# Choice of experts in five pieces in the head of the second attention, the drain of the first in another order, later weights at other addresses

## The reference, cut to what matters

```python
# first attention: 16 heads, delta rule (state += k * beta*(v - k.state)), then
x = x + _L0_attn_ref(xn, ...) + _L0_ffn_ref(xn, ...)      # the latter: 2 of 8 experts for each token
xn = _layernorm(x, axis=-1)
# second attention: for each chunk of 64 tokens, for each sequence and head
gate = ki @ w0_; hb = ki @ w2_; hidden = silu(gate) * hb
dhidden = vi @ w1_.transpose(0, 2, 1)
w1g = newtonschulz5(einsum(hidden * lr1i, vi))            # two steps: A = X X'; B = bA + cAA; X = aX + BX
w0g = newtonschulz5(einsum(ki * lr0i, silu_backprop(dhidden * hb, gate)))
w2g = newtonschulz5(einsum(ki * lr2i, dhidden * silu(gate)))
# w += wg, columns scaled back to their first norms; oi = silu(qi @ w0_) * (qi @ w2_) @ w1_
# lr0, lr1, lr2 = softplus(x @ W_lr + b_lr + const)
# second feed-forward part
gate_probs = softmax(x.mean(axis=1) @ gate_W.T)           # 8 x 6
topk_vals, topk_idx = top_k(gate_probs, 2); topk_vals /= topk_vals.sum()
```

## Time and profile before

| | us |
|---|---|
| median of 3 runs | 1823.56 (1822.08 to 1824.55) |
| the profiled execution | 1825.56 |
| its span, first to last instruction | 1823.8 |
| TensorE busy | 1708.1 (94%) |
| VectorE busy | 1491.5 (82%) |
| ACT busy | 1199.8 (66%) |
| GpSimd busy | 1102.9 (60%) |

### The profile page before, as it was taken

The page is one execution under the profiler, slowest core; times in us unless marked ns, Lnnn a source line. Parts: engine busy times, 40 slices in busy tenths (PEclk is TensorE's granted clock), DMA queues, the critical chain, the costliest instruction groups (busy, mean ns, idle before and its releaser), DMA issues.

```text
span 1823.8 us, 41456 instructions
## 1 busy us (share of the span) xinstructions
PE 1708.1 (94%) x14070; PEld 1242.4 (68%) x14070; DVE 1491.5 (82%) x3496; ACT 1199.8 (66%) x2907; POOL 1102.9 (60%) x1148
## 2 busy tenths in 40 slices
PE   5999899999999999999999999999988778888878
PEld 4477557777777777677777767777767566666666
DVE  4422499999999999999999999999976688888843
ACT  1124467777777777777777777777753678777853
POOL 1510057777777777766666666666666568777831
PEclk8999999999999999999999999999986899999989
DMA  9323300110110101100001000000002000000032
GB/s 308 132 94 110 109 22 27 36 34 26 29 35 20 38 26 29 38 17 26 23 17 29 23 17 23 27 14 29 15 1 59 1 1 2 1 1 1 9 87 81
DMA packets 66096, 73.83 MB, mean 40 GB/s; under 512 B 10975, under 2 KB 54767, under 8 KB 65775
## 3 DMA queue, kind: packets, MB, share of 16 engines
q1 hardware_dynamic: 62919, 63.92, 12.1%
q0 software_dynamic: 3072, 8.65, 1.5%
HBM read 55.45 MB, written 17.10 MB: 40 GB/s over the span
## 4 chain that ended last, share of the span: by engine, by line
PE 83%; DVE 8%; ACT 5%; issue 2%; POOL 1%; SPq 1%; DMA 0%; ACTq 0%; POOLq 0%; DVEq 0%
PE banks L731 19%; PE banks L874 6%; PE banks L743 4%; PE banks L830 3%; PE banks L751 3%; PE banks L849 3%; PE banks L759 3%; PE banks L788 3%; PE banks L802 3%; PE banks L684 3%; PE banks L796 2%; PE banks L930 2%; PE banks L795 2%; PE banks L703 2%; PE banks L1006 2%
## 5 line engine op out<-in xcount | busy, mean ns | idle before, releaser
L731 PE MATMUL banks<-xnT,hw 128*128 128x512 f32 x768 | 414.8, 623 | 4.0 <-DVE cv L2011 4.0
L2052 DVE CAST_PREDICATED MM<-lmask,banks 128x512 bf16<-128x512 uint32 x384 | 270.9, 705 | 36.8 <-PE banks L796 32.3
L2011 DVE SCALAR_TENSOR_TENSOR cv<-banks,hc,cv 128x510 f32<-128x510 f32 (+2 forms) x384 | 283.6, 739 | 11.1 <-ACT cv L1427 6.4
L1477 ACT ACTIVATE T<-banks 128x256 bf16<-128x256 f32 x384 | 150.2, 391 | 144.8 <-PE banks L788 142.9
L2648 POOL TENSOR_TENSOR X<-X,yrow 128x512 f32<-128x512 f32 x128 | 163.4, 1277 | 68.4 <-ACT yrow L1509 68.4
L2612 POOL TENSOR_TENSOR kn<-nsum,half_pos 128x4 f32<-128x4 f32 x64 | 65.5, 1023 | 147.9 <-DVE nsum L2023 147.9
L796 PEld LDWEIGHTS banks<-MM,T 128*128 128x128 bf16 x1536 | 104.2, 98 | 64.4 <-issue 48.0
L795 PEld LDWEIGHTS banks<-T,MM 128*128 128x128 bf16 x1280 | 99.1, 97 | 65.4 <-ACT T L1477 63.2
L788 PEld LDWEIGHTS banks<-MM,Gb 128*128 128x128 bf16 x1536 | 79.1, 98 | 93.6 <-DVE MM L2052 54.5
L874 PE MATMUL banks<-ho,OT 128*128 128x256 f32 x512 | 142.7, 402 | 0.0
L2011 DVE SCALAR_TENSOR_TENSOR cv<-banks,hcv,cv 128x510 f32<-128x510 f32 (+2 forms) x192 | 140.9, 734 | 1.3 <-ACT cv L1427 1.2
(11 more groups left out here) (318 smaller groups left out, 4891.0 us busy)
## 6 DMA issues: line engine op xcount, KB each, us to landing
MM<-in_eye SPq DMA_DIRECT2D x64, 256.0 KB, 2.7
slot_rows<-zeros SPq DMA_DIRECT2D x1, 5304.0 KB, 21.0
xs<-slot_rows SPq DMA_DIRECT2D x13, 408.0 KB, 4.0
slot_out<-ye SPq DMA_DIRECT2D x13, 384.0 KB, 2.7
hw<-in_hw SPq DMA_DIRECT2D x16, 256.0 KB, 3.5
wT<-in_winit SPq DMA_DIRECT2D x8, 384.0 KB, 4.4
wgu<-in_wgu SPq DMA_DIRECT2D x1, 2816.0 KB
w1c<-in_ew SPq DMA_DIRECT2D x16, 176.0 KB
```

The costliest lines, as they stand in the source:

```text
L731: ins = pe.matmul(PROJ[t][:], hw[:, kk, t, :], xnT[:, kk, u.b * BLK:(u.b + 1) * BLK], start=(kk == 0), stop=(kk == KD - 1))
L1477: act.activation(strips(T1[:].rearrange("p i t -> p (i t)"), LEVELS[lv], 0, 1), grams_bank(u)[:, 0:TILES * 64].rearrange("p (k e) -> p k e ...
L2011: dve.scalar_tensor_tensor(o, y, taps_of(t)[:, TAPS - 1 - i:TAPS - i], o, ALU.mult, ALU.add).then_inc(dve_conv, 1)
L2052: dve.copy_predicated(dst, m, ps).then_inc(dve_mm, 1)
```

## The change

Five things are changed.

1. `choose_experts` is cut into `choose_probabilities`, `choose_ranks`, `choose_expert(k)` and `choose_weights`. They are called in the head, among the last VectorE lines before the loop over `pair_period`, and no longer in the loop.
2. ACT's exponential and the Silu behind it become `gate_exponentials`, called between `keep_v(x1)` and `keep_hidden(x1)`; before, they stood last in the head, behind `keep_total(x1)`.
3. The order of the drain and the head is another in some places on all four engines.
4. The weights of pairs 2 and 3 are laid out over buffers of the first attention in another order, and `MM`, `T1` stand behind `hw`, `hc`, `hcv` in memory.
5. SyncE waits for `outputs` and for the squares of unit a62, not for a63, before `load_weights(2)`; the wait for `pe_y` before `load_weights(3)` is gone.

```diff
-        MM = asb("MM", [P, NBLK, 2, TILES, P], BF16)
-        T1 = asb("T1", [P, TILES, P], BF16)
         hw = asb("hw", [P, KD, 3, HD])
         hc = asb("hc", [P, 2, TAPS])
         hcv = asb("hcv", [P, 1, TAPS])
+        T1 = asb("T1", [P, TILES, P], BF16)
+        MM = asb("MM", [P, NBLK, 2, TILES, P], BF16)
...
-        places = [(1, small + early), *((p, small + passing + lasting) for p in range(2, NP)), (1, late), (0, small + passing + lasting), (1, lasting)]
+        places = [(1, small + early), (2, small), (3, these(w02)), (2, turned), (3, small), (2, these(w02) + gated + these(wT) + solved),
+                  (3, turned + gated + these(XX, Bm, w1p)), (3, these(wT, LA)), (1, these(XX)), (0, small + passing + lasting), (1, lasting)]
...
# SyncE
-            sp.wait_ge(pe_solve, 12 * UNITS)
+            sp.wait_ge(pe_solve, 12 * (UNITS - 1))
+            sp.wait_ge(pool_osum, UNITS - 1)
             load_weights(2)
-            sp.wait_ge(pe_y, 2 * UNITS)
             sp.wait_ge(*weights_loaded(2))
             load_weights(3)
# TensorE
             times_gram(a62, 1, 1)
+            project_v(x0)
             invert(a63, 11)
             correct(a62, 1, 1)
             invert(a63, 12)
-            project_v(x0)
             outputs(a62)
# ACT
+            def gate_exponentials():
+                act.wait_ge(*f_lg)
+                act.activation(lge[:], lg[:], ACT.Exp).then_inc(act_once, 1)
+                act.activation(table[:, 1:2], onw[:], ACT.Silu)
...
             square_qk(x0)
+            silu_v(x0)
             invert(a63, 6)
             finish_inverse(a63)
-            silu_v(x0)
...
             keep_qk(x1)
             keep_v(x1)
+            gate_exponentials()
             keep_hidden(x1)
...
             keep_total(x1)
-            act.wait_ge(*f_lg)
-            act.activation(lge[:], lg[:], ACT.Exp).then_inc(act_once, 1)
-            act.activation(table[:, 1:2], onw[:], ACT.Silu)
# VectorE: choose_probabilities, choose_ranks, choose_expert(k), choose_weights hold the steps
# of choose_experts unchanged and in their order
...
             invert(a63, 2)
+            weight_norms()
             second_rhs_half(a62)
             second_rhs(a62)
             invert(a63, 3)
-            weight_norms()
             residual(a62, 1, 0)
             invert(a63, 4)
             refine(a62, 1, 0)
             rates_begin(0)
+            norm_stats(1, 1)
             invert(a63, 5)
             residual(a62, 1, 1)
-            norm_stats(1, 1)
+            sum_qk(x0)
             refine(a62, 1, 1)
-            sum_qk(x0)
             rates_end(0)
+            norm_rows(1, 1)
             residual(a63, 0, 0)
-            norm_rows(1, 1)
+            norm_qk(x0, 0)
             refine(a63, 0, 0)
             square_sums(a62)
             residual(a63, 0, 1)
-            norm_qk(x0, 0)
-            refine(a63, 0, 1)
             norm_qk(x0, 1)
             norm_qk(x0, 2)
+            refine(a63, 0, 1)
             second_rhs_half(a63)
...
             scale(x0, 0)
             scale(x0, 1)
+            choose_probabilities()
             grad_gate(x1)
             grad_hidden(x1)
+            rates_end(3)
             silu_slope(x1)
+            choose_ranks()
             through_silu(x1)
-            rates_end(3)
+            choose_expert(0)
             newton(x0, 0, 0, SQUARE)
+            choose_expert(1)
             sum_qk(x2)
+            choose_weights()
             newton(x0, 0, 0, NEXT)
             norm_qk(x2, 0)
             for n in range(3, STEPS):
                 pair_period(n)
-                if n == 4:
-                    choose_experts()
# GpSimd
             inverse_rms(a62)
+            rate_keys(x0)
             add_rows(a62, 0)
-            rate_keys(x0)
...
             root_grads(x0)
             rate_keys(x1)
+            rate_powers(3)
             one_minus(x1)
             rate_hidden(x1)
-            rate_powers(3)
             root_qk(x2)
```

More of the change, by code:

```diff
@@ L316, in build, with these @@
         lasting = ((wT, "wT", [NM, 4, P], F32), (w02, "w02", [4, 2, P], F32))
-        late = tuple(t for t in passing if t[0] is XX)
-        early = tuple(t for t in passing if t[0] is not XX)
-        places = [(1, small + early), *((p, small + passing + lasting) for p in range(2, NP)), (1, late), (0, small + passing + lasting), (1, lasting)]
+        def these(*group):
+            return tuple(t for g in group for t in passing + lasting if t[0] is g)
+        turned = these(QR, vv, qkT, vT)
+        gated = these(th, sg1, hb1, dgate)
+        solved = these(XX, Bm, w1p, LA)
+        early = these(QR, vv, qkT, vT, th, sg1, hb1, dgate, Bm, w1p, LA)
+        places = [(1, small + early), (2, small), (3, these(w02)), (2, turned), (3, small), (2, these(w02) + gated + these(wT) + solved),
+                  (3, turned + gated + these(XX, Bm, w1p)), (3, these(wT, LA)), (1, these(XX)), (0, small + passing + lasting), (1, lasting)]
         below = [t for p, tensors in places[:-2] for t in tensors]
@@ L2118, in _, with choose_probabilities @@
                     period(h, j)
-            def choose_experts():
-                def by_batch(v):
-                    return v.unsqueeze(2).to_broadcast([1, NB, E1])
+            def choose_probabilities():
                 dve.wait_ge(*f_exp)
@@ L2126, in choose_experts, with choose_ranks @@
                 step(dve.reciprocal(lmx[:], lmx[:]))
-                step(dve.tensor_tensor(lge[:], lge[:], by_batch(lmx[:]), ALU.mult))
+                step(dve.tensor_tensor(lge[:], lge[:], lmx[:].unsqueeze(2).to_broadcast([1, NB, E1]), ALU.mult))
+            def choose_ranks():
                 four = [1, NB, E1, E1]
```

13 lines of the change are left out of this document (7 added, 6 removed).

## The result

The changed kernel takes 1814.53 us, median of six runs (1812.96 to 1817.92); the kernel before, beside it, 1824.05 (1822.08 to 1824.94). The profiled execution took 1812.96 us, with a span of 1811.2 against 1823.8.

What follows compares the result with a forecast made beforehand. The prediction took a closed cycle of waits between engines as the bound, one period lengthened by the choose_experts block. -6.80 (period) + 2.0 (head) - 0.5 (drain) = -5.3 us, from 1823.56 to 1818.3 us; range 1815.0 to 1822.0.

Steps and rivals of the forecast that it cites:

- The period, -6.80: Second attention's periods: taking the choose_experts block out shortens one period from 27.34 to 20.54 us, -6.80 us.
- The 0.84 put down to the lower clock: Part of the period's 6.80 us beyond the 5.96 block: TensorE resuming at its lower clock level, 0.84 us.
- GpSimd and VectorE in the head: Head: GpSimd's earlier power frees rates_end(3), held up 0.95 us beside GpSimd; SQUARE of x0 +1.9, NEXT +3.3 us.
- The table loads: Head, activation engine: loads move behind keep_v(x1), delay keep_hidden(x1) 0.86 us, TURN unchanged; 1.34 us wait for keep_qk(x2) goes.
- The 3.6 us estimated from the Trainium skill's drain: Head: by the skill's load and drain times, two table switches would hold up keep_hidden some 3.6 us; not used in the sum.
- The head costs 2.0 us: Head before the periods: the choice's pieces delay turn_v(x2), and gates(x2) behind it, by 2.0 us.
- slower: Rival: TensorE's longer wait leaves it at 1.2 GHz through head and first periods; +8.5 us, 1832.1; chance 0.03.
- The mark that was set: Sign: keep_v(x1) to project_qk(x3), 32.04 us before; near 34 means the forecast, over 36 costlier-head or slower-clock rivals.
- the first rival: Head hides all the moved work: GpSimd doesn't hold up VectorE, keep_qk's wait pays the rest; -7.0 us, 1816.6; chance 0.17.
- The drain, -0.5: Drain: reordering brings the refinement 0.6 to 0.9 us sooner, then TensorE's queue sets the pace; -0.5 us, bounds -1.2 and +1.2.
- The weights, 0: Weights of pairs 2 and 3: loads issue close to 20 us sooner, but nobody waits for them before or after; 0 us.
- The forecast of -5.3: Whole kernel: period, head and drain terms together, -5.3 us, median to 1818.3 us; forecast 1816.5 to 1820, chance 0.58.

Runs made afterwards that it cites:

- e6: Kernel before with only the exponentials moved early, behind keep_v(x1); the choice of experts stays in the period: 1820.79 us, ratio 0.9985.
- e11: Kernel before, unchanged, profiled once more; no median given, its end behind scale(x15, 0) took 87.47 us.
- e12: Kernel before, unchanged, for a second further profile; no median given, its end behind scale(x15, 0) took 84.19 us.
- e1: Kernel before with only the choice of experts, the exponentials and rates_end(3)/rate_powers(3) moved as in the change: 1819.61 us, ratio 0.9954.
- e3: Changed kernel with SyncE's waits before load_weights(2) and (3) as they were, so the weights load late: 1819.99 us, ratio 0.9961.
- e5: Changed kernel once more, unchanged, beside the kernel before on one chip: 1815.06 us against 1823.78, ratio 0.9958.
- e2: Changed kernel with choice, exponentials and rates_end(3)/rate_powers(3) put back; new drain order, addresses and early weights kept: 1830.08 us, ratio 1.0012.
- e4: Changed kernel with TensorE's products for the first SQUARE of x0 made nine times, filling its wait: 1820.23 us, ratio 0.9960.
- e7: Changed kernel with SQUARE of x0 put ahead of the ranks and both experts: ratio 0.9957 to the kernel before.
- e8: Changed kernel with five more small VectorE steps that do nothing behind pair_period(4): 1814.83 us, ratio 0.9959.
- e13: Kernel before with five small VectorE steps that do nothing behind pair_period(6), putting off its end: ratio 1.0012.
- e14: Kernel before with eight small VectorE steps that do nothing behind pair_period(6), putting off its end: ratio 1.0019.
- e10: Like e9, but with rates_end(3) and rate_powers(3) early as in the change: 1812.81 us, ratio 0.9950.
- e9: Changed kernel with the choice's pieces in VectorE's waits of five periods, rates_end(3)/rate_powers(3) put back: 1811.13 us against 1823.01, ratio 0.9936.

## Why the prediction was right in direction and missed in size

- **The period, -6.80: right.** -6.86 from x3 to x15. This section took 293.15 to 293.28 us in the four profiles that have the block and no added steps or late low stretch (before, e6, e11, e12) and 286.36 to 286.44 in four without it (after, e1, e3, e5). In e2, e4 and e7 a low stretch of the head reaches into the first period and adds 0.9 to 1.1 to it. The 0.84 put down to the lower clock went with the block. e8 and e13 show the same form: a pause of TensorE in the periods, then a low stretch.
- **GpSimd and VectorE in the head: right, a little too dear.** In times of before, `rates_end(3)` starts at 1416.73 (forecast 1416.65) and ends at 1420.3 (1420.5). It was held up by 0.64 instead of 0.95, and not in its chain of seven (1.49) but in three single steps beside `one_minus` and `rate_hidden` (the 0.38, 0.33 and 0.47 above; each took 0.18 before, the first in the earlier trace rows). The ranks, with GpSimd idle, took what they took in the block. The Trainium skill ("GPSIMD Engine Reference", "1. Specifications") names VectorE instructions with two SBUF inputs and those in a 2-port perf mode. Of the three that were held up, the 0.33 has two SBUF inputs; the 0.38 and 0.47 have one, and no run here shows in which mode they ran. SQUARE came +1.48 (forecast +1.9) and NEXT +2.85 (+3.3), the second SQUARE at 1434.13 (1434.3), `gates(x2)` +1.66 (+2.0).
- **The table loads: right.** 2.96 us from the first load to `keep_hidden(x1)`, which is 0.89 later (forecast 0.86); TURN at 1415.20 in times of before (1415.16). The 3.6 us estimated from the Trainium skill's drain ("ScalarE: Activation LUTs", "What ACT_TABLE_LOAD costs") are not there: 0.89 was measured. The wait of 1.34 us for `keep_qk(x2)` is gone.
- **"The head costs 2.0 us": the step that failed.** The way from `gates(x2)` to `project_qk(x3)` was put at no change without a reason: the prediction took `gates(x2)` as the start of the cycle and let what follows be as before. The text had the lower clock as a loss only, in the rival "slower"; it did not ask at which level the kernel before ran its own chain. The earlier trace rows showed 1.00 for the windows up to 1424.7 and from 1441.7 on, and the gap between them, where the low stretch of 1435 to 1441.5 lies, was not looked at. (Of the two slices in the earlier trace rows that the prediction names, the 0.6 is the first.) From `gates(x2)` to `project_qk(x3)` it was 7.73 and became 5.58: -2.15 on the +1.66, so -0.5 for the head. Over five profiles of each (before, e11 to e14; after, e1, e3, e5, e8) the head is 30.60 and 29.99 us on average, -0.6. e6 shows those 2.15 with another cause of the shift, e4 and e7 show 8.30, when the low clock falls there again. Why the low stretches fall where they do stays open. The mark that was set, `keep_v(x1)` to `project_qk(x3)`, is 31.54 against 32.04 before. Under 33 was to mean the first rival; the number is met and its mechanism isn't, since NEXT's delay did reach `gates(x2)`. With e5 and e11 the difference of the heads in a single pair of profiles is anywhere from about -1.5 to +1.1, in no pair +2.0.
- **The drain, -0.5: not settled.** The refinement did come 1.2 us sooner, and `project_qk(x1)` 2.15, counted from the rate bias. But the next matmuls of TensorE need what stands behind GpSimd's power for pair 1, and that was only 0.6 sooner (lines below): TensorE waited 1.72 instead of 0.40, then 3.37 instead of 2.71, and 0.27 was left. Over all nine profiles with the new order (after, e2 to e5, e7 to e10) the drain takes 72.95 to 75.19 us, 74.7 on average with a median of 75.06; over the seven with the old order (before, e1, e6, e11 to e14) 74.99 to 75.40, 75.2 with a median of 75.19. So it is 0.4 by the averages and 0.1 by the medians, and the difference of the two is e4 and e7, which kept more of the lead. The term's path, that TensorE's own queue sets the pace in the end, was not the one that the rows show.
- **The weights, 0: right.** Nobody waits for them in e3 either.
- **The end: no term at all.** -3.80 in the two profiles. The ends with the block in place average 85.3 us (seven executions), those without 83.6 (nine), both reaching from under 84 to over 87. In each the length follows the mean clock: the three ends above 87 us (before, e5, e11) had 0.92, that of e9, 82.28, had 1.00. So most of the 3.8 is luck of the pair of executions. Whether the remaining 1.7 is there on average stays open; e11 to e14 show only that the clock makes it and that the change isn't needed for it.

Put together: -6.9, head about -0.6, drain -0.1 to -0.4, is -7.6 to -7.9. The measured -9.5 has an interval of -11.5 to -6.7, and the other versions with the same lines moved (e1, e3, e5) give -7.8, -7.4 and -8.7. The forecast of -5.3 was short by 2.15 for the clock's part in the head and by small terms; the rest, up to 2 us, is the end, the part ahead of the drain or the spread, and its cause is not shown.

The drain after: VectorE's `refine(a62, 1, 1)`, the last step of `rates_end(0)`, and `norm_rows(1, 1)`, which now stands ahead of the residual (compare); TensorE's wait for that residual (2.72 before); GpSimd's sum of squares beside the last step of `rates_end(0)`.

```profile
1359.84 0.42 DVE L2072 TENSOR_TENSOR Wd<-Wd,banks 128x256 f32<-128x256 f32 x1
...
1363.36 1.19 DVE L2373 SCALAR_TENSOR_TENSOR lr<-lgt,lr 128x24 f32<-128x24 f32 x1
1364.58 1.38 DVE L1882 TENSOR_SCALAR ln_row<-X,ln_mv,ln_rs 128x256 f32<-128x256 f32 x4
```

```profile
1366.35 0.40 PE L808 MATMUL banks<-Rb,MM 128*128 128x128 bf16 x2 [3.36 <-DVE Rb L2066]
```

```profile
1363.24 1.26 POOL L2625 TENSOR_TENSOR Osq<-Osq,sqq 128x512 f32<-128x512 f32 x1
```

Where the lead was lost: GpSimd's `rate_powers(1)`, TensorE's matmul of the squares and its turning of the normalized rows, after and then before.

```profile
1379.67 4.17 POOL L2782 TENSOR_TENSOR lgt<-lgt 128x24 f32<-128x24 f32 x1
...
1385.23 0.63 PE L864 MATMUL banks<-ident,Osq 128*128 128x128 f32 x4 [1.72 <-POOL Osq L2625]
...
1390.95 0.66 PE L591 MATMUL banks<-ident,ln_row 128*128 128x128 f32 x4 [3.37 <-DVE ln_row L1882]
```

```profile
1381.47 4.17 POOL L2765 TENSOR_TENSOR lgt<-lgt 128x24 f32<-128x24 f32 x1
...
1387.24 0.63 PE L858 MATMUL banks<-ident,Osq 128*128 128x128 f32 x4 [0.40 <-POOL Osq L2608]
...
1392.31 0.66 PE L585 MATMUL banks<-ident,ln_row 128*128 128x128 f32 x4 [2.71 <-DVE ln_row L1873]
```

## What to carry to other kernels

A block of small steps in a closed cycle costs its whole length and the slower matmuls behind the pause; cut into pieces of at most 1.6 us, which fit the wait of 1.86 us that its own engine already has in the cycle, it cost 0.07 us a period, and the kernel was faster than with the block moved to the head (e9). Before pricing a move in a stretch where the clock changes, list at which level each matmul of the chain runs now: the gain or loss there can be as large as the step that is moved. Where the clock's stretches move with every edit, a single profile is no measure of a section; take several before a difference of 1 to 4 us is given a cause.

## What the runs showed of the hardware

- The clock followed more than idle time. TensorE was busy for 20.96 of 22 us between 1391 and 1413 in the changed kernel, with matmuls of 128x6 among others, at a granted clock of 0.54. In e4, filled with matmuls up to 1424, it fell at 1429.5 and stayed at 0.51 for 20.5 us; in the kernel itself, idle for 4.40 us, it was low for 10. These are single executions.
- The same binary met its low stretches at other places in another execution: the head of after took 29.68 and 31.30 us, the end of before 87.72, 87.47 and 84.19. Between runs the time goes with the mean granted clock: in e1, 1824.0 us at 0.975, 1819.5 to 1824.1 at 0.977, 1816.4 and 1816.5 at 0.981.
- An added pause of 1.1 us of TensorE in a period (e13) brought 1.3 us more behind it, as the block of 5.96 had brought 0.84; pieces that left TensorE's waits as they were (e9) brought none.
- Small VectorE steps beside GpSimd had a pattern. Over all 16 profiles, 177 steps of `rates_end` began while GpSimd was in a subtraction, addition or multiplication of tensors of 128x256 or 128x512, and every one of them ended 0.03 to 0.05 us after that instruction, the 23 with one SBUF input (TENSOR_SCALAR) like the 154 with two: the step of 1.19 us from 1363.36 ends at 1364.55, GpSimd's of 1.26 from 1363.24 at 1364.50. 265 began while GpSimd was in a power of 1.01 or 2.27 us and took at most 0.19 us. The 17 reciprocals of `rates_end` that began beside the first kind took their usual 0.30. The chain of seven took 1.48 or 1.49 us in the 16 cases without GpSimd and 1.95 to 2.91 beside it.
